# Fill of a pipelined attention: first gathers moved into the stage before, exponential table loaded at the start, first q and k written in three parts, first maxima turned earlier, idle products on TensorE

## The reference, cut to what matters

```python
x = x + 0.5 * ffn(layernorm(x))      # 8 experts, 128 -> 512 -> 128, gelu; a token goes to its best
                                     # expert, if its rank in its batch is below a capacity
x = x + attn(layernorm(x))           # 16 heads of 8, causal, softmax in float32
x = x + 0.5 * ffn(layernorm(x))

def attn(batch):
    qkv = batch @ (sigma_param / sigma * W_qkv)
    q, k, v = split_heads(qkv)
    att = softmax(where(causal, q @ k.T * hd ** -0.5, big_neg))
    return (att @ v) @ (sigma_param / sigma_proj * W_proj)
```

## Time and profile before

| | |
|---|---|
| median of 3 runs | 1034.62 us (1032.22, 1034.62, 1035.82) |
| the profiled execution's own time | 1035.15 us |
| its span | 1033.3 us |
| busy in the span | PE 896.4 (87%), DVE 724.8 (70%), POOL 682.8 (66%), ACT 607.5 (59%) |
| experts e1 end on TensorE | 276.1 us |
| attention's first instruction | 279.5 us |
| scores by query of batch 0, 1, 2 begin | 304.62, 318.63, 332.43 us |
| main work of batch 1 begins | 340.69 us |

### The profile page before, as it was taken

The page is one execution under the profiler, slowest core; times in us unless marked ns, Lnnn a source line. Parts: engine busy times, 40 slices in busy tenths (PEclk is TensorE's granted clock), DMA queues, the critical chain, the costliest instruction groups (busy, mean ns, idle before and its releaser), DMA issues. The chain is left out here.

```text
span 1033.3 us, 26499 instructions
## 1 busy us (share of the span) xinstructions
PE 896.4 (87%) x8219; PEld 679.6 (66%) x8219; DVE 724.8 (70%) x2368; ACT 607.5 (59%) x1581; POOL 682.8 (66%) x1247
## 2 busy tenths in 40 slices
PE   5937499999647999999999999999999873999995
PEld 5823399999623566565656666565656542999995
DVE  8879745444237889899998989998898845444441
ACT  2637366666313666676666666666666651766662
POOL 7709668643023678888888888888887773355554
PEclk9999799999958999999999999999999985999998
DMA  7450022223145544446354554545454102222220
GB/s 214 128 173 1 17 69 67 69 66 64 40 79 106 122 96 101 115 94 122 95 116 101 109 108 97 121 95 117 95 115 97 39 24 61 60 67 67 64 59 21
DMA packets 127407, 89.72 MB, mean 87 GB/s; under 512 B 14305, under 2 KB 117910, under 8 KB 127270
## 3 DMA queue, kind: packets, MB, share of 16 engines
q1 hardware_dynamic: 103078, 52.69, 22.8%
q10 hardware_dynamic: 15488, 17.74, 7.7%
q0 software_dynamic: 8704, 17.60, 6.6%
HBM read 52.23 MB, written 35.47 MB: 85 GB/s over the span
## 5 line engine op out<-in xcount | busy, mean ns | idle before, releaser
L1291 ACT ACTIVATE at_pt<-at_pm 128x512 f32<-128x512 f32 x384 | 228.5, 598 | 117.9 <-PE at_pm L1379 84.2
L1609 DVE TENSOR_REDUCE at_mx<-at_pp 128x2 f32<-128x512 f32 (+1 forms) x384 | 259.5, 678 | 44.7 <-PE at_pp L1368 37.1
L1207 POOL TENSOR_SCALAR_AFFINE_SELECT at_pt<-at_pt 128x256 f32<-128x256 f32 (+1 forms) x384 | 187.8, 493 | 57.4 <-ACT at_pt L1291 54.1
L925 ACT ACTIVATE e_ht<-e_ps_h,b1t 128x128 f32<-128x128 f32 x576 | 164.8, 370 | 98.2 <-PE e_ps_h L954 98.2
L964 PE MATMUL e_ps_y<-w,e_ht 128*128 x1152 | 159.2, 282 | 0.0
L954 PE MATMUL e_ps_h<-e_xnt,e_w1own 128*128 128x128 f32 x1152 | 154.8, 279 | 1.4 <-issue 1.4
L954 PEld LDWEIGHTS e_ps_h<-e_xnt,e_w1own 128*128 128x128 f32 x1152 | 143.0, 195 | 1.6 <-issue 1.6
L964 PEld LDWEIGHTS e_ps_y<-w,e_ht 128*128 128x128 f32 x1152 | 140.0, 192 | 1.7
L1011 DVE SCALAR_TENSOR_TENSOR e_y<-e_ps_y,e_x 128x256 f32<-128x256 f32 x72 | 30.6, 425 | 155.7 <-PE e_ps_y L964 155.7
L888 POOL DMA_INDIRECT out_dram<-e_y,e_x x72 | 73.6, 1022 | 86.4 <-DVE e_y L1011 74.8
L1400 PE MATMUL at_po<-at_pt,vp 128*32 128x256 f32 (+1 forms) x2048 | 109.8, 332 | 1.6 <-POOL at_pt L1207 1.6
(11 more groups left out here) (327 smaller groups left out, 1788.6 us busy)
## 6 DMA issues: line engine op xcount, KB each, us to landing
at_qkd<-at_part SPq DMA_DIRECT2D x64, 192.0 KB, 3.0
kb<-at_qkd SPq DMA_DIRECT2D x64, 96.0 KB
qs<-at_qkd ACTq DMA_DIRECT2D x64, 96.0 KB
e_x<-buckets SPq DMA_DIRECT2D x72, 66.0 KB, 1.9
x<-e_y SPq DMA_DIRECT2D x36, 128.0 KB, 1.8
rows<-ts_x ACTq DMA_DIRECT2D x16, 264.0 KB, 3.0
ts_x<-in_x_dram SPq DMA_DIRECT2D x16, 256.0 KB, 3.5
x_by_token<-at_xa SPq DMA_DIRECT2D x32, 128.0 KB
```

The costliest lines, as they stand in the source:

```text
L925: last = a.activation(hid_t[j % NB][:, f, :], ps_h[j % NB][:, f, :], ACT.Gelu, bias=c.b1t[:, ds(e, 1), f])
L1207: g.affine_select(out=tile, in_=tile, compare_op=ALU.is_ge, fill=0.0, base=0, pattern=[[0, n], [1, P]], channel_multiplier=-1).then_inc(ma ...
L1291: a.activation(pt[u % RING][:, :], pm[u % 2], ACT.Exp, scale=SCALE).then_inc(exped, 1)
L1609: v.tensor_reduce(out, src, axis=AX.X, op=ALU.max).then_inc(maxed, 1)
```

## The change

The change touches the end of route's buffers, the end of experts e1, and the fill of attention.

1. xa and its semaphores move to `consts`. At the end of experts e1, GpSimd waits until all of y_dram has landed and gathers batch 0's two tiles there; attention's own gathers begin with batch 1. To make room, route's at_p lies in the four qs buffers.
2. ScalarE runs one exponential of a single element at the start of attention, so that the table of the exponential is loaded there.
3. For batch 0, q and k are written to qkd in three parts: slots 0 and 5 after a_done, slots 1 and 4 after b_done (two DMAs each on SyncE), slots 2 and 3 after part_done (one half on SyncE, one on ScalarE in step 8). Both readers also wait for the new semaphore.
4. In turn -1 the maxima of batch 0 are turned on TensorE in step 5, ahead of the scores of batch 1, and copied by ScalarE in step 5, not 8; SyncE puts them into qs ahead of the writes of batch 2's q and k. v of that turn waits for the copy, since both use the same bank.
5. Idle products: `identb` times `mask`, 128 x 512 bf16, whose results nobody reads. 12 at the end of experts e1 (both stages of experts have the code, only e1 takes it), 10 at the start of turn -4, 8 in front of step 5 of turn -2, 10 in front of step 5 of turn -1.

```diff
+    c.xa = [m.sb(f"at_xa{k}", [P, TPB, D + 2]) for k in range(2)]
+    c.xa_in = [m.sem(f"at_xa_in{k}") for k in range(2)]
...
-        at_p = sb("atp", [P, NT, P], BF16)
+        at_p = [q[:, :, :].rearrange("p h s -> p (h s)").rearrange("p (n w) -> p n w", w=P) for q in c.qs]
...
                     if j % 2 == 1 and 3 <= j // 2 < 3 + 4 * NQ:
                         blank(j // 2 - 3)
+                for k in range(NR):
+                    pool.wait_ge(y_out[k], OUTS * len(range(k, NU, NR)))
+                for j in range(TPB):
+                    pool.indirect_dma_start(c.xa[0][:, j, 0:D], None, y_dram,
+                                            bass.IndirectOffsetOnAxis(ap=c.place[:, j:j + 1], axis=0)).then_inc(c.xa_in[0], 16)
...
                         contract(j, e[j % IDS])
+            if by_slot:
+                for n in range(12):
+                    te.matmul(ps_h[0].rearrange("p f n -> p (f n)"), c.identb[:, :], c.mask[:, :, :].rearrange("p a q -> p (a q)"),
+                              start=True, stop=True, skip_group_check=True)
...
+        BUSY = {-4: (0, 10), -2: (5, 8), -1: (5, 10)}
...
                     n, h = b + 3, (k + 1) % 2
-                    wait(sp, part_done, n + 1)
...
+                    if n == 0:
+                        for done, s in ((a_done, slice(0, 6, 5)), (b_done, slice(1, 5, 3))):
+                            wait(sp, done, 1)
+                            for r in range(2):
+                                sp.dma_start(rows_out(h, r)[:, s, :], part[h][64 * r:64 * r + 64, s, :]).then_inc(piece_out, 16)
+                        wait(sp, part_done, 1)
+                        sp.dma_start(rows_out(h, 0)[:, 2:4, :], part[h][0:64, 2:4, :]).then_inc(part_out[h], 16)
+                    if b == -1:
+                        maxima_in(b, k)
+                    if n > 0:
+                        wait(sp, part_done, n + 1)
...
                 if has(3):
                     wait(sp, part_out[h], dma_count(n, 2, 2)(h))
+                    if n == 0:
+                        wait(sp, piece_out, 64)
...
-                    if u in (2, 3) and has(4):
+                    if u in (2, 3) and has(4) and b + 4 > 0:
...
+            a.activation(cell[0:1, 7:8], c.part[0:1, 0:1], ACT.Exp, scale=-1.0).then_inc(early_exp, 1)
             act.wait_ge(zeroed, NZ)
...
-                    if u == 8 and has(1):
+                    if u == 8 and b == -3:
+                        wait(act, part_done, 1)
+                        act.dma_start(rows_out(0, 1)[:, 2:4, :], part[0][64:P, 2:4, :]).then_inc(part_out[0], 16)
+                    if u == (5 if b == -1 else 8) and has(1):
...
+                def busy(times):
+                    for n in range(times):
+                        te.matmul(po, c.identb[:, :], c.mask[:, :, :].rearrange("p a q -> p (a q)"),
+                                  start=True, stop=True, skip_group_check=True)
...
                     if u == 5 and has(3):
                         wait(pe, r_done, b + 4)
+                        if b == -1:
+                            wait(pe, mt_out, b + 2)
...
                 for u in range(NP):
+                    if b in BUSY and u == BUSY[b][0]:
+                        busy(BUSY[b][1])
+                    if b == -1 and u == 5:
+                        wait(pe, r_done, b + 4)
+                        turn_maxima()
                     for o, v in QUERY_TILES[u]:
```

More of the change, by code:

```diff
@@ L643, in invert @@
                 for n in range(g * TG, (g + 1) * TG):
-                    last = te.matmul(ps_inv, at_p[:, n, :], at_t[:, :, n, :],
+                    last = te.matmul(ps_inv, at_p[n // PN][:, n % PN, :], at_t[:, :, n, :],
                                      start=(n == 0), stop=(n == NT - 1), skip_group_check=True)
@@ L1061, in attention @@
         SCALE = HD ** -0.5
-        xa, xr, x2 = two("xa", [P, TPB, D + 2]), two("xr", [P, TPB, D]), [sb(f"x2{k}", [P, TPB, XW]) for k in range(NQ)]
+        xa, xr, x2 = c.xa, two("xr", [P, TPB, D]), [sb(f"x2{k}", [P, TPB, XW]) for k in range(NQ)]
         bn, vare = two("bn", [P, TPB, 6]), two("vare", [P, TPB])
@@ L1081, in attention @@
         qkd = [nc.dram_tensor(f"at_qkd{k}", (6 * P, S), BF16, kind="Internal").ap() for k in range(2)]
-        xa_in, xr_in = ([sem(f"{n}{k}") for k in range(2)] for n in ("xa_in", "xr_in"))
+        xa_in, xr_in = c.xa_in, [sem(f"xr_in{k}") for k in range(2)]
         row_out = [sem(f"row_out{k}") for k in range(NQ)]
@@ L1159, in turn @@
                     n, h = b + 3, (k + 1) % 2
-                    wait(sp, part_done, n + 1)
[L1161 to L1169, removed]
+                    if n == 0:
[9 more added lines that the diff above has]
+                        wait(sp, part_done, n + 1)
+                        wait(sp, main_done, (n - NQ + 1) * NP)
+                        wait(sp, qk_in[(k + 1) % NQ], dma_count(n - 2, NQ, 12)(k + 1))
+                        for r in range(2):
+                            sp.dma_start(rows_out(h, r), part[h][64 * r:64 * r + 64, :, :]).then_inc(part_out[h], 16)
+                if has(1) and b > -1:
+                    maxima_in(b, k)
                 if has(3):
                     wait(sp, part_out[h], dma_count(n, 2, 2)(h))
+                    if n == 0:
+                        wait(sp, piece_out, 64)
                     q, src = (k + 3) % NQ, qkd[h].rearrange("(a g) n -> a g n", g=HP)
@@ L1403, in times_v, with turn_maxima @@
                     last.then_inc(pv_done, 1)
+                def turn_maxima():
+                    wait(pe, mp_done, b + 2)
+                    for j in range(TPB):
+                        last = te.transpose(mi[0].bitcast(BF16)[0:3 * H, j * P:(j + 1) * P],
+                                            mp[(k + 1) % 2][:, j, :, :].rearrange("p t h -> p (t h)"), c.identb[:, :])
+                    last.then_inc(mt_tr, 1)
+                def busy(times):
+                    for n in range(times):
+                        te.matmul(po, c.identb[:, :], c.mask[:, :, :].rearrange("p a q -> p (a q)"),
+                                  start=True, stop=True, skip_group_check=True)
                 def small(u):
@@ L1477, in small @@
                         last.then_inc(proj_mm, 1)
-                    if u == 8 and has(1):
-                        wait(pe, mp_done, b + 2)
+                    if u == 8 and has(1) and b > -1:
                         wait(pe, v_out, b + 4, B)
                         wait(pe, num_out, b - 1)
[L1482 to L1485, removed]
+                        turn_maxima()
                 for u in range(NP):
+                    if b in BUSY and u == BUSY[b][0]:
+                        busy(BUSY[b][1])
+                    if b == -1 and u == 5:
+                        wait(pe, r_done, b + 4)
+                        turn_maxima()
                     for o, v in QUERY_TILES[u]:
```

20 lines of the change are left out of this document (15 added, 5 removed).

## The result

| | median | runs |
|---|---|---|
| before | 1033.86 us | 7 (1032.22 to 1036.55) |
| changed | 1041.41 us | 7 (1038.26 to 1043.94) |

The ratio is 1.0068, with a 95% interval of 1.0049 to 1.0086: 7.0 us slower, 5.1 to 8.9 with the interval, where 2 us faster had been forecast. (The two medians lie 7.6 us apart; the ratio is what the text goes by.) A second measurement on another chip gave 1.0058 (1.0045 to 1.0071), 4.7 to 7.4 us. The profiled execution's span is 1039.7 us, 6.4 more than before.

A forecast was written before the change was run, and what follows sets the result against it. The chain of kb waits in attention's fill was taken as the bound; 1.4 (shift of a_done) + 0.7 (parts) + 0.1 - 0.2 (links) = 2.0 us off 1034.62 gave 1032.6, with an 8-in-10 range of 1029.4 to 1036.2.

The forecast's parts named there:

- The gathers: Batch 0's gathers moved to the end of e1: statistics 1.44 us earlier, though attention begins 2.5 us later.
- The products of turn -4: 10 idle products ahead of batch 0's turned rows: delay 0.6 us (0 to 1.1), upper-clock gain 0.6.
- The three parts: Batch 0's q and k written in smaller pieces land earlier: gain 0.7 us, ends 0.1 and 1.2.
- The links: Scores of batch 0 to 1, then 1 to 2: first gains 0.1 us, second costs 0.2.
- The serial chain: Three waits for kb in the fill, links of 14.01 and 13.80 us; gains off this chain end in the last wait.
- The table: Exponential's 1.28 us load moved early: no gain, since TensorE then waits longer for kb before batch 2's scores.
- Rival C: Gathers wait longer at e1's end or small pieces land no sooner: 0 to 1 us left, 1034.1; chance 0.13.
- Rival B: Idle products at the lower clock delay real ones in turns -4, -2, -1: +2.5 us, 1037.1; chance 0.10.
- Its sign: Batch 0's first matmul starts right behind the last idle product, not behind VectorE; no size given.

The follow-up runs named there:

- experiment 1: The changed kernel with batch 0's gathers back in attention, the rest of the change kept; ratio to the kernel before 0.9996 (0.9987 to 1.0006).
- 6: The kernel of experiment 1 without the early exponential, so the table loads late again; ratio to the kernel before 0.9997 (0.9988 to 1.0006).
- 7: The kernel of experiment 1 with all idle products left out; ratio to the kernel before 0.9998 (0.9988 to 1.0008).
- 8: The kernel of experiment 1 with batch 0's maxima turned late, in step 8 of turn -1; ratio to the kernel before 1.0026 (1.0014 to 1.0038).
- w3_best: The changed kernel with batch 0's gathers first in attention, maxima late, idle products 24, 6, 10, 8 in turns -4, -2, -1, 0; ratio to before 0.9982.
- 2: The kernel before with only the gathers moved to the end of e1 (and at_p in the qs buffers); ratio 1.0050 (1.0033 to 1.0066).
- 3: The changed kernel with batch 0's gathers reading input x, without waiting for y_dram; ratio to the kernel before 0.9972 (0.9959 to 0.9985).
- 4: The changed kernel with one of batch 0's gathers at the end of e1, the other in attention; single run, 1051.14 us beside 1043.64.
- 5: The kernel of experiment 1 with 8 more idle products in front of step 5 of turn 0; ratio to the kernel before 0.9999 (0.9989 to 1.0009).

## Why the prediction was wrong

**The gathers: the step that failed.** It put the second gather's end at 281.0 and from there 1.0 us to attention's first instruction, a gain of 1.44 at the statistics. The pace of the two came as worked out (279.94 and 281.19, 1.25 apart), the first of them 0.5 us later than worked out, beyond the 0.65 by which e1 ended later in that run. The way through the barrier didn't come so: it takes 6.8 us from the gather's end to attention's first instruction, not 1.0, since the drain ends 6.1 after it. The statistics came 12.60 us after e1's last tile, not 7.95, so the term was +4.65 and not -1.44. The 1.0 was read from a barrier that GpSimd had reached with its drain long over the earlier trace rows. An indirect DMA was put in front of the barrier that ends a stage, and GpSimd's drain behind it was put at nothing, without a reason.

**The products of turn -4: inside its range.** Turned rows 0.7 us late (3.11 against 2.42 after the statistics; 0 to 1.1 forecast, 0.6 taken), and the clock rose in time for wq and wk, 1.1 in place of 2.07. That the range held is in part luck: it was worked out for a pause of 3.25 us in front of the products, and the pause was 9.66. In experiment 1, with the gathers back, the clock did not rise in time.

**The three parts: right, size a little off.** From a_done (295.20) to the first read (300.00) 4.80 us, before 5.81: a gain of 1.0, where 0.7 was taken and 1.2 was the end. The last piece landed 2.1 us after its issue (297.90 to 300.00), where 2.4 was taken.

**The links: as forecast, but within the spread.** Scores of batch 0 follow the last of the 8 products without a gap (305.30 and 308.71), 8.71 us after the first read of kb, where 8.36 stood before. The link to batch 1 is 13.81 against 14.01, the second 13.98 against 13.80, near the 0.1 and 0.2 forecast; in the second pair of traces both links are the same with and without the change (13.94 and 13.92, 13.49 and 13.49). The serial chain held in every kernel: 27.4 to 28.7 us from scores 0 to scores 2 in twelve of fourteen traces, the two others (29.5 and 29.6) with batch 2's writes late.

**The table: no gain, as said, but the next step was missing.** I wrote that the 1.28 us would end in the wait for batch 2, and the traces agree: that wait was 2.2 us with the early load in 1 and 1.05 without it in 6. I did not ask what a wait of 2.3 us does to the clock, though I had priced just that at the three other places. Behind it the distance to turn 1 grew from 9.37 to 10.79. Together with 1.2 won up to the scores of batch 2 this left +0.2 for the whole fill behind the statistics. So in the traces the rest of the change cancels itself; in the times of experiment 1 it is a gain of 0.4 with an interval of -0.6 to 1.4, and the runs don't tell the clock's share in it.

**Rival C** named the right place, gathers that "wait longer at the end of e1", and bounded it at a lost gain. **Rival B** gave a slowdown by another mechanism. Its sign is there, a first matmul of batch 0 right behind the last idle product (292.50 in the changed kernel), and so are products in the way in experiments 7 and 8, worth up to 1 us each. But they are not the cause of the loss: with all 40 of them kept and only the gathers back the loss was gone. The sum for the changed kernel with the drain in it would have been +4.65 - 1.2 + 1.4 = +4.9 against the first trace of before.

## What to carry to other kernels

Before an instruction is moved in front of a barrier, read what the barrier itself costs on that engine: the drain rows of each queue over the whole trace, those that end long before the barrier above all, because their price shows only when the cover is gone. An indirect DMA as a stage's last act on GpSimd left some 6 us of bare drain in three kernels here (changed, the gathers alone, one gather early); the same DMAs right behind the barrier cost none (w3_best). And of a gain that ends in a wait, ask what the longer wait sets off: here it was TensorE's clock, and behind a load moved out of the way the traces show a slower turn.

## What was not expected of the hardware

- GpSimd's drain ends 5.9 to 6.3 us after the end of its last indirect DMA at the end of both experts stages in all fourteen traces, with one or two gathers, gathers or scatters, covered or not (among them 282.14 to 288.3; 259.92 to 266.0; 287.64 to 293.7). It is not one fixed time everywhere: at the end of attention, behind the scatters to `buckets`, it ends 3.1 to 3.5 us after the last of them (in the kernel before 866.31 to 869.64). Behind route's tensor instructions it ends within 0.1 us. What it waits for isn't shown. The data had landed long before: attention's statistics in the changed kernel began 0.43 us after its first instruction. At the end of the program the drain stands bare in every kernel: in the one before, SyncE had its last write by 1027.6 and reached the barrier at 1027.8, GpSimd's drain from 1023.8 ended near 1032.3. At most some 4.5 us may lie there, an estimate from these rows; it wasn't tried.
- A pause of 0.94 to 1.25 us before batch 2's scores left TensorE's clock at 1.00 (the two traces of before, 2 and 6), and so did one of 1.95 us (3). One of 2.1 to 2.65 us was followed by a fall to 0.50 in six of six traces (changed, changed again, 1, 4, 7, 8).
- The clock can fall in a stretch without such a pause: in 3, 5, 6 and 8 it went to 0.50 for some 6 us, 6 to 7 us after the scores of batch 0 began, with no pause of TensorE above 0.59 us in between.
